# Attention masks by GpSimd selects after the exponential instead of by mask matmuls, with averages, turns and the next group's preparation in a new order

## What is computed

```python
def sdpa(q, k, v, mask):
    scores = einsum('bhqd,bhkd->bhqk', q, k) / sqrt(HD)          # HD = 8
    scores = where(mask, scores, -1e30)
    return einsum('bhqk,bhkd->bhqd', softmax(scores), v)
...
# global: 16 heads, 4 key/value heads, keys through a latent of 32
q, k = rope(q), rope(k); q, k = qk_norm(q), qk_norm(k)
mask_global = i[:, None] >= i[None, :]
# local: the same with its own weights, window of 32
mask_local  = (i - j >= 0) & (i - j < 32)
x = x + global(rmsnorm(x, w1)); x = x + local(rmsnorm(x, w2))
```

## Time and profile before

| | us |
|---|---|
| median of 3 runs (745.0 to 746.87) | 745.13 |
| the profiled execution, its own time | 744.09 |
| its span, first to last instruction | 742.3 |
| PE, DVE, ACT, POOL busy in the span | 639.4, 581.2, 526.4, 418.6 |
| first and last exponential of the attentions start at | 567.7, 731.1 |

### The profile page before, as it was taken

How to read it: one execution, slowest core, us unless ns; L and a number is a source line. 1 busy time by engine, 2 the same in 40 slices (tenths; PEclk the granted TensorE clock), 3 DMA queues, 4 the chain that set the end, 5 groups by cost and what they waited for, 6 DMA issues and landing times.

```text
span 742.3 us, 14099 instructions
## 1 busy us (share of the span) xinstructions
PE 639.4 (86%) x4851; PEld 468.8 (63%) x4851; DVE 581.2 (78%) x852; ACT 526.4 (71%) x1001; POOL 418.6 (56%) x362
## 2 busy tenths in 40 slices
PE   5899987879889799798997985888999888989896
PEld 3488965657668577576675764876877344445443
DVE  6535769999999999999999999997316556566552
ACT  3455465896978969878789899673544777866673
POOL 5400047999999999999999999992000000000000
PEclk9699999999999999999999998999999999999998
DMA  6313467669688596885877858781110000000000
GB/s 210 114 58 115 147 145 219 208 160 262 182 201 252 158 239 198 183 253 169 193 260 157 250 181 195 228 230 43 57 58 1 2 1 1 2 1 2 15 16 29
DMA packets 81415, 100.18 MB, mean 135 GB/s; under 512 B 32561, under 2 KB 37817, under 8 KB 81345
## 3 DMA queue, kind: packets, MB, share of 16 engines
q1 hardware_dynamic: 81344, 99.29, 48.2%
HBM read 96.12 MB, written 3.24 MB: 134 GB/s over the span
## 4 chain that ended last, share of the span: by engine, by line
PE 50%; DVE 17%; issue 14%; ACT 13%; POOL 4%; DMA 0%; POOLq 0%; DVEq 0%; ACTq 0%
PE ps L1849 5%; DVE hc L1222 4%; DVE ps L1214 4%; PE ps L1827 3%; DVE moe L1214 3%; PE ps L2160 3%; PE ps L1904 3%; PE ps L1919 3%; PE ps L1759 2%; PE ps L1810 2%; PE ps L2133 2%; PE ps L2057 2%; PE ps L2067 2%; PE ps L1779 2%; POOL drive L689 2%
## 5 line engine op out<-in xcount | busy, mean ns | idle before, releaser
L689 POOL TENSOR_TENSOR drive<-dtu,b_sb 128x512 f32<-128x512 f32 x160 | 204.1, 1285 | 1.5 <-DMA b_sb<-bc_rows 1.4
L697 POOL TENSOR_TENSOR hc<-moe,c_sb 128x512 f32<-128x512 f32 x128 | 166.1, 1298 | 8.2 <-DVE moe L1214 8.2
L1214 DVE TENSOR_TENSOR_SCAN moe<-ps,drive 128x512 f32<-128x512 f32 x128 | 153.3, 1198 | 0.7 <-ACT decay_sb L885 0.5
L1849 PE MATMUL ps<-ident,hc 128*128 128x128 f32 x1024 | 134.9, 275 | 3.3 <-POOL hc L697 3.0
L1849 PEld LDWEIGHTS ps<-ident,hc 128*128 128x128 f32 x1024 | 116.6, 142 | 28.6 <-issue 19.3
L885 ACT ACTIVATE ps<-dt,negA 128x510 f32<-128x510 f32 x160 | 106.5, 677 | 28.9 <-DVE moe L1214 28.2
L1214 DVE TENSOR_TENSOR_SCAN ps<-decay_sb,ps 128x512 f32<-128x512 f32 x96 | 117.1, 1220 | 1.2 <-ACT decay_sb L885 1.1
L1121 ACT ACTIVATE probs<-ps 128x1024 f32<-128x1024 f32 (+1 forms) x96 | 86.5, 916 | 35.6 <-PE ps L2133 29.3
L702 POOL TENSOR_TENSOR stat<-stat,halfc 128x4 f32<-128x4 f32 x7 | 7.1, 1008 | 170.8 <-DVE stat L1483 170.8
L1222 DVE TENSOR_TENSOR hc<-ps,c_sb 128x512 f32<-128x512 f32 x128 | 85.2, 666 | 0.0
L885 ACT ACTIVATE decay_sb<-dt,negA 128x510 f32<-128x510 f32 x96 | 68.3, 711 | 16.0 <-DVE ps L1214 16.0
(11 more groups left out here) (282 smaller groups left out, 1191.0 us busy)
## 6 DMA issues: line engine op xcount, KB each, us to landing
b_sb<-bc_rows SPq DMA_DIRECT2D x128, 256.0 KB, 4.2
c_sb<-bc_rows SPq DMA_DIRECT2D x128, 256.0 KB, 4.1
xm<-spot_rows SPq DMA_DIRECT2D x48, 256.0 KB, 4.9
wbuf<-in_pack SPq DMA_DIRECT2D x16, 514.0 KB, 3.5
wbuf<-in_pack SPq DMA_DIRECT2D x8, 512.0 KB, 5.5
spot_rows<-c_sb SPq DMA_DIRECT2D x6, 256.0 KB, 3.6
x_sb<-in_x SPq DMA_DIRECT2D x4, 256.0 KB, 3.8
out<-x_sb SPq DMA_DIRECT2D x4, 256.0 KB, 2.3
```

The costliest lines, as they stand in the source:

```text
L689: pool.tensor_tensor(drive_of(N, half), dtu[:, N // STATES % 2, half], b_sb[:, N % B_RING], ALU.mult) \
L697: pool.tensor_tensor(hc[:, 2 * (N % DEEP) + half], h_of(q), c_sb[:, N % C_RING], ALU.mult).then_inc(sem["hc_pooled"], 1)
L1214: dve.tensor_tensor_scan(h_of(q)[:, turn], decay_bank(q)[:, turn], source[:, turn], 0.0, ALU.mult, ALU.add).then_inc(sem["scan_done"], 1)
L1849: last = pe.matmul(ps[:, Y_BANK + half, block], hc[:, 2 * (N % DEEP) + half, block], ident[:], start=False, stop=True, is_transpose=True, ...
```

## The change

- `hide` (new, on POOL): after the exponential of a diagonal unit, `affine_select` keeps an element of `probs` where query >= key and writes 0 elsewhere. It does so for all four diagonal units of a batch in the global layer, and for the first unit (U even) of each diagonal tile in the local layer, where a second select over 96 keys x 768 columns cuts what is outside the window. These 48 units (32 and 16) have no mask matmuls any more and take 64 selects; the other 16 diagonal units, U odd in the local layer, keep theirs. `average` waits for the selects (`probs_seen`).
- Averages stand at slot 2t + 4, one unit later. `turn` part 2 stands a slot before the batch's first unit, was in it. `back` and `copy` come a slot later, `O1` and `O2` too, `T` one later.
- `rms` of groups 2 to 7 is in two steps, `squares` at -17 and `root` at -15. The power is no longer POOL's but an Ln and an Exp on ACT (128x4).
- The square in `sqr` is DVE's (128x640, both inputs in SBUF), was ACT's.

```diff
-        for part, at in enumerate((-3, -2, 0)):
-            put(6 * b + at + (b == 0 and part == 2), "turn", b, part)
-        put(6 * b + 10, "back", b)
-        put(6 * b + 8, "copy", b)
+        for part, at in enumerate((-3, -2, -1)):
+            put(1 if (b, part) == (0, 2) else 6 * b + at, "turn", b, part)
+        put(6 * b + 11, "back", b)
+        put(6 * b + 9, "copy", b)
...
-        if at % 2 and 1 < at <= UNITS1 + 1:
-            unit.append(("average", at // 2 - 1))
+        if at % 2 == 0 and 2 < at <= UNITS1 + 2:
+            unit.append(("average", at // 2 - 2))
...
+def by_pool(U):
+    return BLOCKS[U // 2 % 3] != (0, 1) and (U // 6 < SEQS or U % 2 == 0)
...
+            def hide(U):
+                pool.wait_ge(sem["probs_ready"], U + 1)
+                p = probs[:, U // 2 % 3, 2 * (U % 2):2 * (U % 2) + 2].rearrange("p g (j q) -> p g j q", j=GROUP)
+                causal = pool.affine_select(p, p, [[0, 2], [0, GROUP], [1, P]], ALU.is_ge, 0.0, base=0, channel_multiplier=-1)
+                if U // 6 < SEQS:
+                    causal.then_inc(sem["probs_seen"], 1)
+                    return
+                causal.then_inc(sem["probs_cut"], 1)
+                pool.wait_ge(sem["probs_cut"], cut_before(U) + 1)
+                far = p[0:P - WINDOW, :, :, WINDOW:P]
+                pool.affine_select(far, far, [[0, 2], [0, GROUP], [-1, P - WINDOW]], ALU.is_ge, 0.0, base=-1, channel_multiplier=1) \
+                    .then_inc(sem["probs_seen"], 1)
...
+                if kind == "root":
+                    act.wait_ge(sem["rms_var"], G)
+                    act.activation(stat[:, 1, rows], stat[:, 2, rows], ACT.Ln).then_inc(sem["rms_ln"], 1)
+                    act.wait_ge(sem["rms_ln"], G - 1)
+                    act.activation(stat[:, 3, rows], stat[:, 1, rows], ACT.Exp, scale=-0.5).then_inc(sem["rms_pow"], 1)
...
-                    act.activation(qk_sqr[:], qk[:, r].rearrange("p h d -> p (h d)"), ACT.Square).then_inc(sem["qk_sq"], 1)
+                    dve.tensor_tensor(qk_sqr[:], qk_row, qk_row, ALU.mult).then_inc(sem["qk_sq"], 1)
...
-                    elif kt == qt:
+                    elif kt == qt and not by_pool(U):
...
                 pe.wait_ge(sem["probs_ready"], 2 * t + 2)
+                after(pe, "probs_seen", seen_before(2 * t + 2))
```

More of the change, by code:

```diff
@@ L101 @@
     "rope_a", "roped", "v_ready", "qk_sq", "qk_sum", "qk_var", "qk_ln", "qk_inv", "qk_normed", "qk_hi", "qk_split",
[L102 removed]
+    "turn_q", "turn_copied", "scores_ready", "probs_ready", "probs_seen", "rms_ln", "probs_cut", "av_done", "den_done",
     "ones_ready", "av_copied", "av_turned", "heads_done", "out_ready",
@@ L256, in attention_timeline @@
     for b in range(2 * SEQS):
-        for part, at in enumerate((-3, -2, 0)):
-            put(6 * b + at + (b == 0 and part == 2), "turn", b, part)
-        put(6 * b + 10, "back", b)
-        put(6 * b + 8, "copy", b)
+        for part, at in enumerate((-3, -2, -1)):
+            put(1 if (b, part) == (0, 2) else 6 * b + at, "turn", b, part)
+        put(6 * b + 11, "back", b)
+        put(6 * b + 9, "copy", b)
     for G in range(GROUPS):
-        for name, at in (("rms", -17), ("T", -14), ("L", -12), ("Q", -11), ("K", -9), ("sqr", -8), ("inv", -7), ("split", -6),
-                         ("O1", 19), ("O2", 21)):
+        for name, at in (("T", -13), ("L", -12), ("Q", -11), ("K", -9), ("sqr", -8), ("inv", -7), ("split", -6),
+                         ("O1", 20), ("O2", 22)):
             if name != "L" or G < GROUPS // 2:
                 put(12 * G + at, name, G)
+        if G >= 2:
+            put(12 * G - 17, "squares", G)
+            put(12 * G - 15, "root", G)
+        else:
+            put(12 * G - 17, "rms", G)
     order, readers = [], []
@@ L294, with seen_before, cut_before @@
 PREP = {ev: n for n, ev in enumerate(ev for ev in FILL + AT_ORDER if ev[0] in ("T", "L", "Q", "K", "O1", "O2"))}
+def by_pool(U):
+    return BLOCKS[U // 2 % 3] != (0, 1) and (U // 6 < SEQS or U % 2 == 0)
+def seen_before(U):
+    return sum(by_pool(V) for V in range(U))
+def cut_before(U):
+    return sum(by_pool(V) for V in range(6 * SEQS, U))
 def shared_before(q):
@@ L787, in _ @@
                     rms_pow(ev[1])
+                elif ev[0] == "unit" and by_pool(ev[1]):
+                    hide(ev[1])
         @block.scalar
@@ L1023, in prepare @@
                 rows = slice(GT * k, GT * k + GT)
-                if kind == "rms":
+                if kind == "root":
[3 more added lines that the diff above has]
+                    act.activation(stat[:, 3, rows], stat[:, 1, rows], ACT.Exp, scale=-0.5).then_inc(sem["rms_pow"], 1)
+                elif kind in ("rms", "squares"):
                     if l:
@@ L1038, in prepare @@
                     act.activation(latT[:, cols_k], ps[0:LAT, PREP_BANK], ACT.Copy).then_inc(sem["prep_free"], 1)
-                elif kind == "sqr":
-                    act.wait_ge(sem["roped"], G + 1)
-                    after(act, "qk_sum", G)
-                    act.activation(qk_sqr[:], qk[:, r].rearrange("p h d -> p (h d)"), ACT.Square).then_inc(sem["qk_sq"], 1)
                 elif kind == "inv":
@@ L1538, in prepare @@
                     rms_scale(G)
+                elif kind == "squares":
+                    rms_sums(G)
+                elif kind == "root":
+                    rms_scale(G)
                 elif kind == "Q":
@@ L1567, in prepare @@
                 elif kind == "sqr":
+                    dve.wait_ge(sem["roped"], G + 1)
+                    qk_row = qk[:, r].rearrange("p h d -> p (h d)")
+                    dve.tensor_tensor(qk_sqr[:], qk_row, qk_row, ALU.mult).then_inc(sem["qk_sq"], 1)
                     dve.wait_ge(sem["qk_sq"], G + 1)
@@ L2133, in scores @@
                         last = pe.matmul(ps[:, kv], kT[g, r, kt * P:(kt + 1) * P], qT[g, r, :, qt * P:(qt + 1) * P],
-                                         start=(kt != qt), stop=True)
+                                         start=(kt != qt or by_pool(U)), stop=True)
                 last.then_inc(sem["scores_ready"], 1)
```

1 line of the change is left out of this document (removed).

## The result

The changed kernel takes **751.49 us** (median of 5 runs, 750.79 to 752.34); the kernel before took 745.0 in the same comparison. The ratio is 1.0085, interval 1.0067 to 1.0103: slower by 6.3 us. The forecast of 735.4 was wrong, in sign too, and 751.49 lies outside its range of 727 to 748.

A forecast was written before the change was run, and what follows sets the result against it. PE was taken as nearly the bound (busy 20.7 of 22.8 us a global group), ACT 3.4 us behind. The terms, -10.2 - 5.5 - 1.0 + 4 + 1 + 2 = -9.7 us, gave 735.4 us from the median 745.13; range 727 to 748.

The forecast's parts named there:

- Masks: Mask matmuls of 48 units leave PE: 16.3 us of work, 5/8 of it taken as on the path, -10.2 us.
- Power: Power moves from POOL to ACT, key copy ahead of the scale: PE's waits for that copy go, -5.5 us.
- Square: Square in `sqr` moves from ACT to DVE, so no exponential queues behind it: -1.0 us, bounds 0 and -2.3.
- Selects: Selects on POOL at 1.3 us, no average waiting; contention with DVE's `split` costs +4 us, bounds 0 and +9.
- Order: `T` directly ahead of `L` makes `L` wait for ACT's copy: +1 us; the other later steps cost nothing.
- Clock: With fewer matmuls PE idles more often: one more fall of its granted clock, +2 us, bounds -3 and +10.
- rival C: Each of the eight groups has a clock fall, six more, +10 us: about 745 us, no change; chance 0.09.
- Rivals A and B: A: selects of 3.5 us make POOL the bound, 777 us, chance 0.14. B: selects cost 2.57 us, some 742, 0.17.

The follow-up runs named there:

- e1: The kernel before with the mask matmuls of the 48 units left out and nothing in their place: 740.05 us, ratio 0.9923 to before.
- e16: The changed kernel with the mask matmuls of the 48 units issued as well as their selects: 758.37 us, ratio 1.0159 to before.
- e6: e1 with rms in two steps and the power as Ln and Exp on ACT for six groups: 741.25 us, ratio 0.9937 to before.
- e7: e1 with only the square on DVE instead of ACT: 746.94 us, ratio 1.0010 to before.
- e2: The changed kernel without the selects and the wait for them, 48 units' masks not applied: 745.05 us, ratio 1.0003 to before.
- e12: e6 with selects for all 48 units and the averages waiting for them at their old places: 746.18 us, ratio 1.0016 to before.
- e13: The changed kernel with the square back on ACT and the third turn back in the batch's first slot: 746.09 us, ratio 1.0011 to before.
- e8: e1 with only the third turn a slot earlier and T a slot later: 748.48 us, ratio 1.0036 to before.
- e10: The changed kernel with only the third turn back in the batch's first slot: 747.50 us, ratio 1.0028 to before.
- e3: e2 with all masks on PE as before, so the new order without selects: 749.71 us, ratio 1.0036 to before.

## Why the prediction was wrong, term by term

- **Masks (-10.2).** Mis-sized: 5.7 (e1) and 5.5 (e16) were gained. The 5/8 read from one chain counted PE's order, not what PE does with a shorter one: it stands idle longer (3.6 to 4.7 us a group for 2.1) and is granted a lower clock.
- **Power (-5.5).** Failed: "The 5.5 us of PE's waits go". In the changed kernel they are 7.7. The key copy does stand ahead of the scale, but the term looked at DVE's order alone: the copy is still behind the sums, and on PE `O2`, the average and `back` that covered it went behind the turn that needs it. With these in the old places the wait is gone (e6), and still nothing is gained (+1.0), so the wait was not 5.5 us of the path either. The part is worth 9.6 once POOL has selects, by a path that no term had.
- **Square (-1.0).** Wrong in sign: +2.3 in the change, +6.5 alone. "DVE's takes its place in the same line" priced it at 0.85 us against ACT's 0.73. The price was right (0.82 in e7 and e2, 0.99 beside selects), but it stands in DVE's queue with the copies for which PE waits.
- **Selects.** Price right (1.22 us for 1.3), no average waits in the change; contention booked +4, bounds 0 and +9, measured +6.1 (e2) and +5.9 (e6 to e12). `split` was the right place but not the only one: the scales and the residual add are stretched as well. (The forecast's aside that a select of 0.9 us would make the term "about 3" does not follow from its own working: the keys would be ready after 1.3 us, within the 1.4 of cover, and the term near 0.)
- **Order (+1).** Failed. T costs about 2.2. The third turn, a slot earlier, was put at nothing without a reason and costs 4.2. "Keep their distances and cost nothing" missed the later averages both ways: +29 in the old order, a gain of 6.5 in the new. It also missed what they take from PE between the turns (the power's term).
- **Clock (+2).** Windows under 1.00 appear in the global layer, the sign that was named for rival C (six more falls, +10), and lost clock in the profiles rose by 11.7 us. Rival C's total, 745, did not come, since the other terms did not hold. How much of the time is the clock's is not shown. It is not to be added to the terms measured by removal, which already hold their share of it.

In sum, one part after the other from the kernel before to the change: masks out -5.7 (e1), root on ACT +1.0 (e6), 48 selects +5.9 (e12), `T` and the averages with all that follows them -0.4 (e13), square and third turn +5.5 (the change), together the measured +6.3. That it adds up is no proof, since each part is the difference of two runs and good to 2 or 3 us; in another order the parts come out otherwise, the averages above all. Against the forecast's -9.7 it is 16.0 us: 6.5 from the power, 6.5 from the square with the third turn, 4.5 from the masks, 1.9 from the selects, less 1.4 from `T` and the averages and the 2 booked for the clock. Rivals A and B fell with the price; the slower side needed no dear select, only steps that move in two queues at once.

Open: how much of each moved step is clock and how much is waiting. e8 had a low lost clock (7.9) and was still 8.4 us above e1, and e10 gained 4.2 at nearly the change's lost clock, so the clock is not the whole of it. Open too: which part of the change makes the later averages a gain, and why the third turn costs.

## What to carry to other kernels

Work taken off the busiest engine is worth at most what the next wait leaves over, and perhaps less again if that engine's clock then falls; before a removal is priced, ask what the engine will do in the time. Price every moved step in every queue that it passes, and look on both sides of a wait: a copy that comes earlier gains nothing if the work that covered the wait moves behind it. Judge a set of moves together as well as one by one: the later averages cost 29 us alone and gained 6.5 in company, while the best version took the smallest part, selects only where nobody waits for them, and moved nothing but the root.

## What the runs showed of the hardware that was not expected

- An in-place select of 128x1024 f32 on POOL takes 1.10 us in the median of 48, cheaper than POOL's own product of 128x512 at 1.285.
- Two meet and both lose: a select beside the residual add took 3.14 us, and the add 3.12 instead of 2.28. The estimate "DVE stands still until POOL is done" does not cover that POOL is held up too. Of the three selects the first still took 1.09 us; the second, which starts while the add runs, took 3.14 and ends some 0.9 us after the add, as if it had stood still for it.
- More PE work went with a faster clock in all three pairs that differ by the 16.3 us of mask matmuls: lost clock 4.3 against 11.0 us (before, e1), 7.9 against 17.9 (e3, e2), 9.8 against 16.0 (e16, change), one profile each, and the mean granted clocks in the same direction.
